# All four row blocks of the last step go through every expert instead of being sorted

## What is computed

```python
h = layernorm(x)
q, k, v = mlp_q(h), mlp_k(h), mlp_v(h)            # 256 -> 256 (gelu) -> 256
scores = tril(q @ k.T / sqrt(256 * 512))          # causal, no softmax
x = x + layernorm(scores @ v) * ln_w + ln_b
idx = argmax(pe @ sign(tile_sigs).T, -1)          # (2048,), 0..7, from the position alone
x = x + (layernorm(x) @ W[idx].T + b[idx])
```

## Time and profile before

| what | us |
|---|---|
| median of 3 runs (lowest to highest) | 312.41 (311.78 to 313.0) |
| the profiled execution, its own time | 312.93 |
| its span, first to last instruction | 311.2 |
| TensorE matmuls busy | 289.2 (93%) |
| VectorE busy | 237.7 (76%) |
| ScalarE busy | 189.0 (61%) |
| GpSimd busy | 176.7 (57%) |

### The profile page before, as it was taken

One profiled execution on the slowest core, in us unless ns is written; L12 is line 12 of the kernel. 1 busy time (PEld: TensorE's weight loads), 2 busy tenths in 40 slices (PEclk: granted clock), 3 DMA queues, 4 the chain that ended last, 5 costly groups with the idle time before them and its releaser, 6 DMA issues.

```text
span 311.2 us, 5456 instructions
## 1 busy us (share of the span) xinstructions
PE 289.2 (93%) x1806; PEld 254.4 (82%) x1806; DVE 237.7 (76%) x539; ACT 189.0 (61%) x380; POOL 176.7 (57%) x238
## 2 busy tenths in 40 slices
PE   8999998998999999999999999999999995788991
PEld 6789887997898989889788988898988984677870
DVE  5769788899889978967995896788587687245661
ACT  2565775776676876776678658769675436053410
POOL 6881532370685568475737545584577578545552
PEclk9999999999999999999999999999999999579997
DMA  7909950012021120121031000260224413911110
GB/s 223 233 22 333 350 175 27 0 37 66 0 75 67 36 72 2 68 70 39 10 127 54 20 0 2 73 199 2 88 95 134 154 58 127 312 53 67 50 42 17
DMA packets 24209, 27.83 MB, mean 89 GB/s; under 512 B 4659, under 2 KB 22068, under 8 KB 24118
## 3 DMA queue, kind: packets, MB, share of 16 engines
q1 hardware_dynamic: 15910, 13.68, 14.7%
q0 software_dynamic: 3296, 8.64, 8.0%
q10 hardware_dynamic: 4976, 5.16, 4.9%
HBM read 13.95 MB, written 14.44 MB: 91 GB/s over the span
## 4 chain that ended last, share of the span: by engine, by line
PE 79%; DVE 11%; issue 4%; ACT 3%; POOL 1%; ACTq 0%; POOLq 0%; DVEq 0%
PE ring L493 42%; PE o_ps L493 11%; PE s_ps L493 6%; PE w_ps L493 5%; PE ring L502 2%; PE ring L521 2%; PE sc_ps L606 2%; PE ring L764 1%; ACT xn L986 1%; PE sc_ps L764 1%; PE sc_ps L604 1%; DVE xnT L1166 1%; DVE st L1152 1%; DVE xres L1245 1%; PE w_ps L649 1%
## 5 line engine op out<-in xcount | busy, mean ns | idle before, releaser
L493 PE MATMUL ring<-xnT,w_sp 128*128 128x512 f32 x288 | 73.5, 399 | 3.7 <-DVE hT L1171 1.7
L493 PEld LDWEIGHTS ring<-xnT,w_sp 128*128 128x128 f32 x288 | 51.9, 189 | 16.0 <-issue 3.4
L892 ACT ACTIVATE ring<-ring,b_cols 128x512 f32<-128x512 f32 x48 | 31.7, 660 | 27.2 <-PE ring L493 25.8
L493 PE MATMUL ring<-hT,w_sp 128*128 128x512 f32 x192 | 46.7, 397 | 0.2 <-DVE hT L1171 0.2
L1171 DVE TENSOR_TENSOR hT<-ring,hT 128x512 fp32r<-128x512 f32 x48 | 32.5, 681 | 14.0 <-ACT hT L895 12.3
L493 PEld LDWEIGHTS ring<-hT,w_sp 128*128 128x128 f32 x192 | 35.2, 188 | 8.8 <-DVE hT L1171 0.9
L1717 POOL DMA_INDIRECT sorted_rows<-xres,slot_i x30 | 31.2, 1039 | 8.5 <-issue 6.5
L1782 POOL DMA_INDIRECT out_dram<-slot_rows x22 | 22.0, 999 | 17.6 <-DVE slot_rows L1464 12.0
L1683 POOL TENSOR_TENSOR vtok<-v,vtok 128x512 fp32r<-128x512 f32 x14 | 17.9, 1289 | 24.5 <-ACT vtok L912 24.5
L895 ACT CAST hT<-ring 128x512 fp32r<-128x512 f32 x48 | 28.2, 587 | 1.5
L1245 DVE SCALAR_TENSOR_TENSOR xres<-cen,rs,xres 128x256 f32<-128x256 f32 x32 | 24.1, 762 | 1.9 <-issue 1.6
(11 more groups left out here) (241 smaller groups left out, 683.7 us busy)
## 6 DMA issues: line engine op xcount, KB each, us to landing
sorted_rows<-blank ACTq DMA_DIRECT2D x1, 5032.0 KB, 20.8
xt<-x SPq DMA_DIRECT2D x7, 512.0 KB, 3.4
slot_rows<-sorted_rows SPq DMA_DIRECT2D x22, 136.0 KB
w_stage<-tile_w SPq DMA_DIRECT2D x8, 256.0 KB, 3.3
h<-sorted_rows SPq DMA_DIRECT2D x15, 136.0 KB
xt<-x SPq DMA_DIRECT2D x2, 256.0 KB, 3.0
hT<-position_table POOLq DMA_DIRECT2D x1, 512.0 KB, 9.4
sorted_rows<-xres,slot_i POOLq DMA_INDIRECT x30
```

The lines of the kernel that those rows point to most:

```text
L493: last = te.matmul(o, lhs[k][a], rhs[k][c], start=start and k == 0 and i == 0, stop=stop and k == n - 1 and i == 2, skip_group_check=check)
L892: nc.scalar.activation(full, ring[(2 + m) % 3][:, :], ACT.Gelu, bias=b1c[:, m // 2, m % 2:m % 2 + 1]).then_inc(gelu, 1)
```

## The change

`DENSE` goes from 2 to 4: chunks 0 to 3 of step 7 stay unsorted. `SLOTS` goes from 37 to 35 and `PAIRS` from 18 to 17. The two scatters of the last step go, and block 21 then waits for no scatter that block 17 did not wait for. There are 16 groups in the place of 8, and four plain output DMAs in the place of two. The unsorted chunks are now two pairs (`PAIRS` and `PAIRS + 1`), with places 10 and 11; `LATER` goes from 12 to 10. Pair 10 has place 12, and so on. The transposes of a pair now stand one loop pass ahead of its products' pass. The second unsorted pair uses the other half of `kT`.

TensorE after pair 9: two groups, pair 10, then for m = 11 to 16 one group, transposes of pair m + 1 (while m is below 16) and the products of m, then eight groups with nothing between them.

```diff
@@ -49,12 +49,12 @@
 ROW = C + 16
 
 
-DENSE = 2
+DENSE = 4
 SLOTS = NB * NJ - DENSE + NT - 1
 FIRST = (STEPS - 2) * CH - NT + 1
 EARLY = (STEPS - 1) * CH - NT + 1
 
-AMID, INNER, MIDDLE, LATER = 1, 5, 8, 12
+AMID, INNER, MIDDLE, LATER = 1, 5, 8, 10
 CLASSES = PER
 NOWHERE = 2 * NB * T
 FILLS = 14
@@ -310,7 +310,7 @@
 
         def place(m):
 
-            return m if m < LATER else LATER if m == PAIRS else m + 1
+            return m if m < LATER else LATER + m - PAIRS if m >= PAIRS else m + 2
 
         def pair_t(p):
             if p < MIDDLE:
@@ -322,8 +322,8 @@
 
         def pair_xb(m, a):
 
-            if m == PAIRS:
-                return kT[:, 0].rearrange("p k n -> p (k n)")[:, a * GT:a * GT + GT]
+            if m >= PAIRS:
+                return kT[:, m - PAIRS].rearrange("p k n -> p (k n)")[:, a * GT:a * GT + GT]
             if m < MIDDLE:
                 at = (m + 1) % 2 * 2
                 return xb_all[:, at:at + 2].rearrange("p r a n -> p (r a n)")[:, a * GT:a * GT + GT]
@@ -682,15 +682,18 @@
             def dense_products(e, g):
 
                 i = NT // 2 * e + g
-                if i == 0:
-                    te.wait_ge(xb_lo, AMID + LATER + 1)
+                if i % NT == 0:
+                    te.wait_ge(xb_lo, AMID + LATER + 1 + i // NT)
                 if i < 2:
                     te.wait_ge(o_cen, CH * STEPS)
                 else:
                     te.wait_ge(dense_done, 2 * (i - 1))
-                mm3(o_ps[i % 2][:, :], [[pair_xb(PAIRS, a)[:, cols(2 * e + k)] for a in range(2)] for k in range(KC)],
+                mm3(o_ps[i % 2][:, :], [[pair_xb(PAIRS + e // 2, a)[:, cols(e % 2 * 2 + k)] for a in range(2)] for k in range(KC)],
                     [[wf[:, a, k, 2 * g * C:2 * g * C + 2 * C] for a in range(2)] for k in range(KC)]
                     ).then_inc(dense_ps, 1)
+
+            def dense_group(i):
+                dense_products(i // (NT // 2), i % (NT // 2))
 
             def last_scores(j):
 
@@ -860,18 +863,21 @@
             pair_products(7)
             pair_transposes(9)
             pair_products(8)
+            pair_transposes(10)
             pair_products(9)
-            pair_transposes(10)
+            dense_group(0)
             pair_transposes(11)
+            dense_group(1)
+            pair_transposes(12)
+            pair_transposes(13)
             pair_products(10)
-            pair_transposes(12)
-            pair_products(11)
-            for m in range(LATER, PAIRS):
-                pair_transposes(m + 1)
-                dense_products((m - LATER) // 4, (m - LATER) % 4)
+            for m in range(11, PAIRS):
+                dense_group(m - 9)
+                if m < PAIRS - 1:
+                    pair_transposes(m + 3)
                 pair_products(m)
-            for i in range(PAIRS - LATER, NT):
-                dense_products(i // 4, i % 4)
+            for i in range(PAIRS - 9, DENSE * NT // 2):
+                dense_group(i)
 
         @block.scalar
         def _(act):
@@ -1113,15 +1119,16 @@
             pair_rounded(8)
             pair_norm(9)
             pair_rounded(9)
-            pair_norm(10)
-            pair_rounded(10)
-            pair_norm(11)
-            pair_rounded(11)
             pair_norm(PAIRS)
             pair_rounded(PAIRS)
+            pair_norm(PAIRS + 1)
+            pair_rounded(PAIRS + 1)
+            pair_norm(10)
+            pair_norm(11)
             for m in range(LATER, PAIRS):
-                pair_norm(m)
                 pair_rounded(m)
+                if m + 2 < PAIRS:
+                    pair_norm(m + 2)
 
         @block.vector
         def _(dve):
@@ -1478,6 +1485,11 @@
                 nc.vector.scalar_tensor_tensor(out=dense_rows(e)[:, 0:C], in0=o_ps[i % 2][:, t % 2 * C:t % 2 * C + C],
                                                scalar=onehot[:, t, j:j + 1], in1=dense_rows(e)[:, 0:C],
                                                op0=ALU.mult, op1=ALU.add).then_inc(dense_done, 1)
+
+            def dense_pair(i):
+                e, g = i // (NT // 2), i % (NT // 2)
+                dense_out(e, 2 * g)
+                dense_out(e, 2 * g + 1)
 
             def last_masked(j):
                 dve.wait_ge(scores, CH * LAST + (2, 1, 3, 3)[j])
@@ -1619,27 +1631,27 @@
             pair_out(6)
             pair_rest(7)
             x1_final(LAST, (2, 3))
+            pair_rest(8)
             x1_stats(LAST, (2, 3))
             x1_var(LAST, (2, 3))
             pair_out(7)
-            pair_rest(8)
+            pair_rest(9)
             pair_out(8)
-            pair_rest(9)
+            pair_rest(PAIRS)
             pair_out(9)
+            dense_pair(0)
+            pair_rest(PAIRS + 1)
+            dense_pair(1)
             pair_rest(10)
             pair_rest(11)
             pair_out(10)
-            pair_rest(PAIRS)
-            pair_out(11)
-            for m in range(LATER, PAIRS):
-                pair_rest(m)
-                g = m - LATER
-                dense_out(g // 4, g % 4 * 2)
-                dense_out(g // 4, g % 4 * 2 + 1)
+            for m in range(11, PAIRS):
+                dense_pair(m - 9)
+                if m < PAIRS - 1:
+                    pair_rest(m + 1)
                 pair_out(m)
-            for g in range(PAIRS - LATER, NT):
-                dense_out(g // 4, g % 4 * 2)
-                dense_out(g // 4, g % 4 * 2 + 1)
+            for i in range(PAIRS - 9, DENSE * NT // 2):
+                dense_pair(i)
 
         @block.gpsimd
         def _(pool):
@@ -1819,11 +1831,10 @@
             rstd_out(LAST, (0, 1))
             slots((11, 12))
             rstd_x1(LAST, (0, 1))
-            rows_sorted(LAST, (0, 1))
             rstd_out(LAST, (2, 3))
-            slots((13, 14))
+            slots((13,))
             rstd_x1(LAST, (2, 3))
-            slots(range(15, SLOTS))
+            slots(range(14, SLOTS))
 
 
 def position_table(seq, dim):
```

## The result

The changed kernel takes 314.91 us (median of 5 runs, 314.21 to 315.5), the kernel before 312.41 (5 runs beside them, 311.78 to 313.0). The ratio is 1.0075, with an interval of 1.0052 to 1.0097: slower by 2.5 us, where 314.0 was predicted. The profiled execution took 314.81 with a span of 313.0. On another chip the same code came out level with before (first experiment), which is a part of the story.

What follows compares the result with a forecast made beforehand. Only the end from about 260 us, where TensorE waits and its clock falls, had anything to win. Median 312.4 + 0.3 for TensorE's later end + 1.3 for one low clock stretch = 314.0 us, range 311.0 to 316.0.

Steps and rivals of the forecast that it cites:

- likeliest case: End of the program: one short low stretch of TensorE's clock, kernel slower at 314.0 us, chance 0.40.
- Steps A and B: GpSimd's earlier power to group 0: pair 8's products at 261.35 (3.2 us won), unsorted transposes 264.7, group 0 266.8.
- Step C: Second unsorted pair's transposes to pair 10's products at 272.9: TensorE waits of 0.5, 0.7 and 0.9 us.
- The clock: TensorE between 264 and 280: one short low stretch, priced at 1.3 us, with bounds of 0 and some 5.
- full clock rival: TensorE's waits are too short or too spread for the clock to fall: 312.7 us, chance 0.28.
- Step D: Last loop from group 2 at 274.3: 3.2 us a pass with transposes, then eight groups, 11.3 us, to 304.4.
- The end: TensorE ends at 304.6 against 304.35; output scatters are done by then, and the last DMA hangs on the last group.
- 0.3 predicted: TensorE's end in the new order at full clock: 304.6 against 304.35, 0.3 us later.
- faster rival: Hand-offs from pair 8 to pair 10 overlap better, about half the 4.2 us of waits goes: 310.6 us, chance 0.12.
- floor of 308.5: The time without any of the 4.2 us of TensorE waits laid out from pair 8 to pair 10's products.

Runs made afterwards that it cites:

- first experiment: The changed kernel run once more without any edit, on another chip: 311.23 us (12 runs) against 312.02 for before, ratio 0.9976.
- Step A alone: Kernel before, with GpSimd's power of chunks 2 and 3 ahead of its two scatters and VectorE's rest of pair 8 ahead of the statistics: 310.51 us.
- steps A and D: Kernel before with GpSimd's power ahead of its two scatters and last-loop transposes one place ahead of their products, two chunks still unsorted: 307.23 us, ratio 0.9856.
- last experiment: Changed kernel with both unsorted pairs behind pair 11 and a small GpSimd power behind every second scatter from block 14 to the last: 306.53 us, ratio 0.9813.

## Why the prediction was right, and where only the sum was

The time (314.91 for 314.0) and the sign of the likeliest case were right, but that the number came out is partly luck: an end of the program 3.5 us shorter than laid out was cancelled by a late cast (1.85), by 1.2 us lost ahead of the change and by 0.6 of small terms. On another chip the same kernel was 0.8 under before. Along its steps, for the profiled execution against that of before (VectorE's end 5.34 us later, the span 1.8 longer):

- **Steps A and B** came out within 0.3 us at every place of the table. Step A alone on the kernel before is worth 1.6 us at the end (310.51), half of the 3.2 us by which pair 8's products move.
- **Step C** was wrong at its last instruction: "ScalarE ... then pair 10's cast, to 272.1". The cast came 1.89 us after the norms had ended, pair 10's products 1.85 late. The hand-off I had laid out does hold when GpSimd's scatters are held back or spaced (271.87 and 271.59, no idle time; shown by two runs). What I had left out is that GpSimd, freed of the step's last two scatters, sends seven output scatters in a row just there; before it had four at the most. I read GpSimd only for its powers. The trace of before has what looks like the same in small, which the prediction doesn't mention. Behind its row of four scatters from 278.25 to 283.05 a cast starts 1.42 us after its transposes and not 0.63, and TensorE then waits 0.86 us at 285.37. The timelines of GpSimd (the last of the four), TensorE and ScalarE of the kernel before:

```profile
282.08 0.97 POOL L1782 DMA_INDIRECT out_dram<-slot_rows  x1 [0.30 <-issue]
282.50 0.60 PE L764 MATMUL ring<-ident,xn 128*128 128x128 f32 x4
283.92 0.59 ACT L1013 CAST xnT<-ring 128x512 fp32r<-128x512 f32 x1 [2.84 <-PE ring L764]
```

- **The clock** was right in kind: one short low stretch, after eight transposes in some 4 us. It cost 280.40 - 275.95 - 2.93 = 1.5 us for 1.3; in the same kernel again the stretch was twice as long (273.5 to 280.4) and cost 2.6. That it hangs on the wait ahead of pair 10's products is shown by the profile in which eight matmuls fill that wait, and by the two in which the cast was in time and the wait 0.62 us: none of the three has a low stretch there. The full clock rival (0.28) is as real: on another chip nine of twelve executions were at 310.5 to 311.5, under its 312.7 mainly because of the end. The argument for it, that no wait is as long as the 3.00 us of before, didn't hold: the longest wait was 2.63 us, in the same kernel again 1.82, and the clock fell in both.
- **Step D** was 3.27 for 3.20, 0.4 us in six passes; eight groups took 11.49 us, as counted.
- **The end** was the second missing term, in the other direction. "The last DMA hangs on the last group as before" is wrong: before, the span ended 5.7 us after VectorE, now 2.2. The sum took the 5.7 over without asking what made them. In all fourteen profiles the span ends 2.1 to 2.2 us after VectorE's last result or, where it is later, 5.6 to 5.9 us after GpSimd's last scatter has been issued (before 305.32 to 311.2; step A alone 302.42 to 308.3; steps A and D 298.84 to 304.7; without the last chunk's groups 300.08 to 305.7). With eight groups behind the last pair the scatter is out of the way, 3.5 us.

Together: 0.3 predicted, 1.2 that this execution had lost before 256, 1.85 of step C, 1.5 clock, 0.4 loop make 5.25 of the 5.34; less 3.5 at the end 1.8. The same sum gives the profile without a low stretch, that with the eight matmuls: 0.3, 0.5 lost before 256, 1.05 of step C (its cast was 0.8 less late), 0.4, less 3.5 is -1.25, and its span is 1.2 under that of before (310.0 against 311.2). The medians on that chip differ by 0.8 (311.23 against 312.02).

The faster rival named the right place with the wrong cause. Its floor of 308.5 was too high, as it held the long end too: the last experiment, another order of the same work in which TensorE has no wait left behind 260, has 306.53.

Open: how GpSimd's scatters hold the other engines (the trace says only "remote"; no run separates GpSimd's own work in issuing them from their transfers), from what length of a row on (some rows of four made a cast 0.8 or 1.1 us late and others none; seven made one cast 1.1 to 1.9 late, eight two casts 2.0 and 3.2, nine two casts 3.4 and 4.2, fourteen one by 9.6; but five behind eight spaced ones also made one 2.4 late, so it isn't the count alone), and why the changed kernel took over 314 us in all five runs on one chip and in two of twelve on another.

## What to carry to other kernels

Before moving work, list what each engine will do back to back in the new order, also the engine that is off the path: a queue that is set free can hurt more by its bursts than by its length. If an engine waits with operands ready and the profile names no releaser on the core, look at what GpSimd issues at that time, and try spacing its indirect DMAs to the rate at which they are needed. Powers behind the first eight or ten alone weren't enough here, as GpSimd fell behind and made up for it in a row later. And read the end of the program for itself: two chains may end there, and lengthening one can be free while the other is longer.

## What the runs showed of the hardware

- While GpSimd issued a row of indirect DMA scatters of 128 rows, 0.97 us each with 0.30 between, ScalarE stood beyond its operands for 3.4 and 4.2 us (nine in the row) and once 9.6 us (fourteen), VectorE for up to 3.70 us, and TensorE behind them. With one 0.74 us instruction after every two scatters no such wait was left (314.36 to 306.53 in the same order).
- In fourteen profiles the program ended 5.6 to 5.9 us after GpSimd had issued its last scatter or 2.1 to 2.2 us after the last result of VectorE, which a plain output DMA of SyncE sends, whichever was later.
- TensorE's clock (granted 0.50, the 1.2 GHz level) fell for 3.4 us in one profile of the changed kernel and for 6.8 in the other, the first time behind 4.6 us with only eight transposes to do, the second time 3 us into such a stretch; and not when eight matmuls filled the wait (2.10 us) or when the wait was 0.62 us.
